# Row statistics one chunk ahead, the row factors spread by transposes of a repeated column, and a reordered start and end of stage 1 in a fused attention and dense block

## The reference

```python
def layernorm(x): m = mean(x); v = var(x); return (x - m) / sqrt(v + 1e-5)

# attention on xn = layernorm(x)
C_q  = xn @ Wq_d + bq_d            # 1024 -> 12
C_kv = xn @ Wkv_d + bkv_d          # 1024 -> 4
q = (C_q @ W_qk + b_qk).reshape(b, s, 32, 4)
scores = einsum('bqhd,bkd->bhqk', q, C_kv) / sqrt(4)
attn = softmax(scores)
V = (C_kv @ Wv_u + bv_u).reshape(b, s, 32, 32)
x = x + einsum('bhqk,bkhd->bqhd', attn, V).reshape(b, s, 1024) @ Wo + bo

# dense layer on layernorm(x)
base = layernorm(x) @ W.T + bias
lora = sum_n (2 * lora_weights[n]) * (layernorm(x) @ A[n].T) @ B[n].T   # 8 x rank 16
x = x + base + lora
```

## Time and profile before

| quantity | value |
|---|---|
| median of 3 runs | 2078.73 us |
| the profiled execution, its own time | 2079.62 us |
| its span | 2077.6 us |
| mean granted clock of TensorE | 0.999 |
| ScalarE busy | 1969.5 us (95%) |
| TensorE busy | 1962.2 us (94%) |
| VectorE busy | 475.6 us (23%) |
| GpSimd busy | 214.9 us (10%) |
| first exponential of attention starts | 105.78 us |

### The profile page before, as it was taken

How to read it: one execution, slowest core, us unless ns; L and a number is a source line. 1 busy time by engine, 2 the same in 40 slices (tenths; PEclk the granted TensorE clock), 3 DMA queues, 4 the chain that set the end, 5 groups by cost and what they waited for, 6 DMA issues and landing times.

```text
span 2077.6 us, 36033 instructions
## 1 busy us (share of the span) xinstructions
PE 1962.2 (94%) x15085; PEld 715.1 (34%) x15085; DVE 475.6 (23%) x1140; ACT 1969.5 (95%) x2185; POOL 214.9 (10%) x220
## 2 busy tenths in 40 slices
PE   7979898999999999999999999999999999999999
PEld 4522222333333333333333333333333333333337
DVE  7713333111121211211121111212111111212115
ACT  5799999999999999999999999999999999999980
POOL 5600000000110002000110001100110001100022
PEclk9999999999999999999999999999999999999999
DMA  8442000000010001000010000100010000100011
GB/s 308 147 137 86 3 26 26 5 25 13 26 35 15 13 26 46 5 13 26 26 35 3 26 25 13 36 15 26 13 46 5 26 13 26 35 15 13 26 41 41
DMA packets 45806, 77.42 MB, mean 37 GB/s; under 512 B 15886, under 2 KB 29766, under 8 KB 45642
## 3 DMA queue, kind: packets, MB, share of 16 engines
q1 hardware_dynamic: 43296, 75.02, 10.7%
q10 hardware_dynamic: 2346, 0.09, 0.1%
HBM read 51.23 MB, written 23.86 MB: 36 GB/s over the span
## 4 chain that ended last, share of the span: by engine, by line
ACT 43%; PE 35%; issue 16%; DVE 0%; DVEq 0%
ACT probs L634 43%; PE ps L914 17%; PE ps L959 10%; PE ps L903 6%; PE ps L948 2%; PE ps L937 0%; PE ps L943 0%; PE ps L775 0%; DVE y L1433 0%; PE ps L1056 0%; PE ps L1052 0%; DVE o_t L1489 0%; ACT o_t L649 0%; ACT o_sb L646 0%; DVE recip L1481 0%
## 5 line engine op out<-in xcount | busy, mean ns | idle before, releaser
L634 ACT ACTIVATE probs<-ps 128x1024 f32<-128x1024 f32 x2048 | 1899.8, 1030 | 17.7 <-PE ps L903 7.1
L914 PE MATMUL ps<-probs,c_wide 128*32 128x512 f32 x8192 | 985.7, 599 | 0.0
L903 PE MATMUL ps<-q_in,key_t 27*128 27x512 bf16 x4096 | 404.2, 385 | 94.1 <-ACT probs L634 90.8
L959 PE MATMUL ps<-w_eff,xn_t 128*128 128x512 f32 x1344 | 394.5, 418 | 0.0
L914 PEld LDWEIGHTS ps<-probs,c_wide 128*32 128x32 f32 x8192 | 212.3, 108 | 424.9 <-issue 220.0
L903 PEld LDWEIGHTS ps<-q_in,key_t 27*128 27x128 bf16 x4096 | 103.0, 91 | 722.7 <-ACT probs L634 715.2
L1433 DVE SCALAR_TENSOR_TENSOR y<-ps,nw,y 128x512 f32<-128x512 f32 x64 | 48.1, 751 | 979.0 <-PE ps L959 967.6
L959 PEld LDWEIGHTS ps<-w_eff,xn_t 128*128 128x128 f32 x1344 | 228.2, 188 | 102.1 <-issue 69.8
L536 POOL TENSOR_TENSOR y<-y,ffn_bias 128x1024 f32<-128x1024 f32 x32 | 76.4, 2388 | 1349.9 <-DVEq L1454 1349.9
L531 POOL TENSOR_TENSOR y<-y,attn_bias 128x1024 f32<-128x1024 f32 x32 | 75.9, 2385 | 463.9 <-DMA y<-in_L_attn_x_dram 463.8
L1417 DVE TENSOR_TENSOR y<-ps,y 128x512 f32<-128x512 f32 x56 | 38.7, 692 | 134.9 <-PE ps L937 134.9
(11 more groups left out here) (168 smaller groups left out, 619.7 us busy)
## 6 DMA issues: line engine op xcount, KB each, us to landing
y<-in_L_attn_x_dram SPq DMA_DIRECT2D x40, 512.0 KB, 4.3
out_dram<-y SPq DMA_DIRECT2D x31, 512.0 KB, 2.7
area<-in_L_attn_x_dram SPq DMA_DIRECT2D x16, 512.0 KB, 9.1
q_in<-q_parts SPq DMA_DIRECT2D x256, 27.0 KB
q_parts<-q_parts_sb SPq DMA_DIRECT2D x48, 128.0 KB, 2.8
xn<-in_L_attn_x_dram SPq DMA_DIRECT2D x8, 512.0 KB, 7.7
y<-in_L_attn_Wo_dram SPq DMA_DIRECT2D x1, 2048.0 KB, 8.6
xn<-in_L_attn_Wo_dram SPq DMA_DIRECT2D x1, 2048.0 KB, 13.3
```

The source lines that it names most:

```text
L634: nc.scalar.activation(probs[:, (c * STEPS + step) % PROBS, bass.ts(pair, 2 * N)], ps[:, 2 * (i % SCORE_SLOTS):2 * (i % SCORE_SLOTS) + 2, ...
L903: last = nc.tensor.matmul(ps[:, at, :], key_t[TILE * h:TILE * h + KEYS, bass.ts(b * KT + kt, P)], q_in[TILE * h:TILE * h + KEYS, g % 2, :] ...
L914: last = nc.tensor.matmul(ps[32 * h:32 * h + 32, SUMS, :], c_wide[:, b * KT + kt, at:at + 32], probs[:, (c * STEPS + step) % PROBS, bass.t ...
L959: last = nc.tensor.matmul(ps[:, SHARED, :], xn_t[:, t % 2, a, kb, :], w_eff[:, b, kb, bass.ts(half, N)], start=(kb + i == 0), stop=(kb == ...
```

## The change

The sections of stage 1 are changed as follows.

1. `statistics` runs one chunk ahead instead of two: DVE's loop for c is now `scale_parts(c-1)`, `split_latents(c-2)`, `statistics(c+1)`.
2. POOL no longer builds the diagonal blocks. PE spreads the factors with four transposes in which one column of `x_r` is read as 128 columns. `deviations_x(c)` waits for `r_ps` where it waited for `diag_ready`.
3. For chunk 0 `spread_r` and `move_r` move from the end of chunk 0 to behind block 1 of chunk 1.
4. The largest latent is no longer taken per chunk from `lat`. It is taken once per batch from the turned latents in `c_wide` (`largest_of_rows`), turned on PE (`turn_largest`), reduced again and spread.
5. The nine weight loads are counted by two semaphores: three by `w_in`, six by `wqk_in`. Only the query bias waits for the six.
6. PE runs `keep_busy` transposes at the start: 16 before anything else and 2, 6 and 4 between the tiles of `turn_first`.
7. At the end, the latents are turned before the queries are made, ACT moves the values first, and the last `split_latents` stands behind the flag, beside the last `split_shift`. The stage 1 buffers lie elsewhere within `probs`, so exponential 3 waits for `lat_split` where exponential 0 did.

```diff
             def deviations_x(c):
...
                 pool.wait_ge(x_measured, c + 1)
                 if c >= 2:
-                    pool.wait_ge(diag_ready, c - 1)
+                    pool.wait_ge(r_ps, c - 1)
...
-                    pool.tensor_tensor(r, a, r, ALU.mult).then_inc(p_r, 1)
-                    pool.wait_ge(p_r, n + 6 + 4 * i)
-                if c:
-                    pool.wait_ge(r_ps, c)
-                pool.tensor_tensor(diag[:, :, :], ident[:, :].unsqueeze(1).to_broadcast([P, TT, P]),
-                                   r.unsqueeze(2).to_broadcast([P, TT, P]), ALU.mult).then_inc(diag_ready, 1)
+                    pool.tensor_tensor(r, a, r, ALU.mult).then_inc(p_r if i < 2 else r_ready, 1)
...
             def spread_r(c):
-                pe.wait_ge(diag_ready, c + 1)
+                pe.wait_ge(r_ready, c + 1)
                 pe.wait_ge(high_ready, c)
-                nc.tensor.matmul(ps[:, 5, :], ones[:, :], diag[:, :, :].rearrange("p t n -> p (t n)"), start=True, stop=True
-                                 ).then_inc(r_ps, 1)
+                for t in range(TT):
+                    last = nc.tensor.transpose(ps[:, 5, bass.ts(t, P)], x_r[:, c % 2, 2, t:t + 1].to_broadcast([P, P]), ident[:, :])
+                last.then_inc(r_ps, 1)
...
+            WARM = (2, 6, 4)
+            keep_busy(16, 5, ident)
...
+                    if t < TT - 1:
+                        keep_busy(WARM[t], 5, ident)
...
-        W_IN = 9 * 16
+        W_IN = 3 * 16
+        WQK_IN = 6 * 16
...
+            def query_bias():
+                pe.wait_ge(wqk_in, WQK_IN)
+                nc.tensor.matmul(ps[:, 6, 0:1], wqk_sb[0:32, :], bqk_sb[0:32, 2:3], start=True, stop=True).then_inc(query_ps, 1)
...
+                    if kb == 1 and c == 1:
+                        spread_r(0)
+                    if kb == 4 and c == 0:
+                        query_bias()
...
-                    if kb == KB - 1:
+                    if kb == KB - 1 and c:
                         spread_r(c)
...
             keep_busy(6, 0)
             sum_parts(CHUNKS - 1)
+            keep_busy(5, 0)
+            turn_latents(CHUNKS - 1, 1)
             queries(CHUNKS - 1)
-            turn_latents(CHUNKS - 1, 1)
+            turn_largest(1, 4)
             keep_busy(2, 0)
-            largest(1, 5)
-            keep_busy(4, 0)
+            largest(1, 4)
+            keep_busy(2, 0)
             pe.wait_ge(caug_ready, START + CHUNKS)
             bounds(1, 6)
...
-                if meanwhile:
-                    ch.then(nc.vector.tensor_reduce(c_max[:, bass.ds(c, 1)], src, AX.X, ALU.max, apply_absolute_value=True))
-                    meanwhile()
-                else:
-                    ch.put(nc.vector.tensor_reduce(c_max[:, bass.ds(c, 1)], src, AX.X, ALU.max, apply_absolute_value=True))
...
+            def largest_of_rows(b):
+                dve.wait_ge(caug_ready, START + (b + 1) * CB)
+                nc.vector.tensor_reduce(c_top[:, b, :], c_wide[:, b * KT:(b + 1) * KT, CW:CW + L].rearrange("p t l -> p l t"),
+                                        AX.X, ALU.max, apply_absolute_value=True).then_inc(c_top_ready, 1)
...
             for c in range(1, CHUNKS):
                 scale_parts(c - 1)
-                if c == 1:
-                    statistics(2)
+                if c == CB + 1:
+                    largest(0, 6)
                 if c == CHUNKS - 2:
                     weigh(0, 6)
-                if 2 <= c < CHUNKS - 1:
+                if c >= 2:
                     split_latents(c - 2, c % 2)
-                if c == CHUNKS - 2:
-                    split_latents(c - 1, 1 - c % 2)
-                if c == CB + 1:
-                    largest(0)
-                if c + 2 < CHUNKS:
-                    statistics(c + 2)
+                if c + 1 < CHUNKS:
+                    statistics(c + 1)
+                if c == CB:
+                    largest_of_rows(0)
...
-            split_latents(CHUNKS - 1, 1, lambda: (largest(1), weigh(1, 5)))
+            largest_of_rows(1)
+            largest(1, 4)
+            weigh(1, 4)
...
-            split_shift(P, 6, shift_split, bound_max[:, 1:2], judge)
+            split_shift(P, 6, shift_split, bound_max[:, 1:2], judge, lambda: split_latents(CHUNKS - 1, 1))
```

More of the change, by code:

```diff
@@ L145, in build_block @@
         nw = sb("nw", [P, 2, 4, TT], F32)
-        c_max = sb("c_max", [P, CHUNKS], F32)
-        c_maxb = sb("c_maxb", [P, B], F32)
+        c_top = sb("c_top", [P, B, L], F32)
+        c_most = sb("c_most", [L, B], F32)
         bound_w = sb("bound_w", [P, B, H], F32)
@@ L660, in _, with keep_busy @@
             pe.wait_ge(const_ok, 4)
+            def keep_busy(times, bank, tile=wqk_sb):
+                for _ in range(times):
+                    nc.tensor.transpose(ps[:, bank, 0:P], tile[:, :], ident[:, :])
+            WARM = (2, 6, 4)
+            keep_busy(16, 5, ident)
             def first_weights():
@@ L666, in first_weights @@
                 nc.tensor.matmul(ps[:, 7, 0:1], bias_row, ones[0:1, 0:1], start=True, stop=True)
-                nc.tensor.matmul(ps[:, 7, 1:2], wqk_sb[0:32, :], bqk_sb[0:32, 2:3], start=True, stop=True)
                 last = nc.tensor.matmul(ps[:, 7, 32:32 + KB * 32], ones[:, :], w_down[:, :, :].rearrange("p k n -> p (k n)"),
@@ L727, in queries, with turn_largest @@
                 nc.tensor.matmul(ps[:, 7, :], wqk_sb[:, :], down_part[:, :], start=True, stop=True).then_inc(q_ps, 1)
+            def turn_largest(b, bank):
+                pe.wait_ge(c_top_ready, b + 1)
+                nc.tensor.transpose(ps[0:L, bank, 0:P], c_top[:, b, :], ident[:, :]).then_inc(c_turned, 1)
             def largest(b, bank):
-                pe.wait_ge(c_max_ready, b + 1)
-                if b == B - 1:
-                    pe.wait_ge(high_ready, CHUNKS)
-                nc.tensor.matmul(ps[:, bank, 0:1], sel_latent[:, :], c_maxb[:, b:b + 1], start=True, stop=True
+                pe.wait_ge(c_most_ready, b + 1)
+                nc.tensor.matmul(ps[:, bank, P:P + 1], sel_latent[0:L, :], c_most[:, b:b + 1], start=True, stop=True
                                  ).then_inc(bound_w_ps, 1)
@@ L756, in stage1 @@
                         down(c - 1, 1)
+                    if kb == 1 and c == 1:
+                        spread_r(0)
+                    if kb == 2 and c == CHUNKS - 3:
+                        pe.wait_ge(caug_ready, START + c - 1)
+                        turn_largest(0, 6)
                     if kb == 2 and c == CHUNKS - 2:
@@ L769, in stage1 @@
                         queries(c - 1)
-                    if kb == KB - 1:
+                    if kb == KB - 1 and c:
                         spread_r(c)
-            def keep_busy(times, bank):
-                for _ in range(times):
-                    nc.tensor.transpose(ps[:, bank, 0:P], wqk_sb[:, :], ident[:, :])
             for c in range(CHUNKS):
@@ L791, in _ @@
             pe.wait_ge(min_ready, 1)
-            nc.tensor.matmul(ps[0:1, 4, 0:P], bound_max[:, B:B + 1], ident[:, :], start=True, stop=True).then_inc(tight_ps, 1)
+            nc.tensor.matmul(ps[0:1, 4, 2 * P:3 * P], bound_max[:, B:B + 1], ident[:, :], start=True, stop=True).then_inc(tight_ps, 1)
             keep_busy(4, 0)
+            pe.wait_ge(high_ready, CHUNKS)
             pe.wait_ge(tight_ok, 1)
@@ L1170, in split_shift @@
                 if then:
+                    beside()
                     dve.wait_ge(first_shift, SHIFT_BLOCKS * 16)
@@ L1174, in split_shift @@
                 ch.then(nc.vector.tensor_tensor(rest, shift, parts[:, 0, :], ALU.subtract))
-                if beside:
+                if beside and not then:
                     beside()
```

57 lines of the change are left out of this document (34 added, 23 removed).

## The result

The changed kernel takes 2073.71 us (median of 7 runs, 2071.58 to 2074.32), the kernel before 2079.61 (7 runs): ratio 0.997, 95% interval 0.996 to 0.9979. It is faster by 5.9 us where 14.4 were forecast, and 2073.71 is 0.7 above the range. The profiled execution of after took 2071.58 (span 2069.7), the fastest of its seven, that of before 2079.62 (span 2077.6). About 0.55 of them can be named. In all twelve other traces with the new order of statistics the step from chunk 1 to 2 took 9.17 to 9.21 us, and only in this one 8.62. In those twelve VectorE's last product of `split_latents` takes 1.54 us, beside GpSimd's L513; here it takes 0.75.

What follows compares the result with a forecast made beforehand. Stage 1 before the first exponential was taken as serial to attention, its period set by DVE (9.85 us), PE next (8.98). Gains 5.5 + 3.1 + 4.3 + 0.4 + 0.4 + 0.7 = 14.4 us gave 2064.3, range 2060.5 to 2073.

Steps and rivals of the forecast that it cites:

- chunk 0 to 1: Step of 11.88 us in stage 1: one chunk's statistics instead of two between the `scale_parts`, so 8.8, gain 3.1.
- four steady steps: `sum_parts` of chunks 1 to 5, 39.46 us: falls to 35.2, gain 4.3; ends 1.9 to 5.2.
- step 5 to 6: Stage 1 step of 10.05 us, bound by PE: loses 0.42 of spreading, `turn_largest` adds 0.15 elsewhere; gain 0.4.
- What waits for the later statistics: Query split and store behind later `deviations_x`: both fit, counted zero, 1 us for each kept in the range.
- the second of the two waits named there: ACT's next use of the query buffer at 17.7; six stores issued by 14, landing by 17, little to spare.
- The end: `sum_parts(7)` to first exponential, 10.81 us: maximum of bounds at 5.9 instead of 7.05; gain 0.7, from 0 to 1.7.
- The start: Until `sum_parts` of chunk 0, at 25.53: faster PE and earlier weights bring it to 20.0, 5.5 us earlier.
- The period: Steady chunk step: loops of 8.56 (PE), 8.6 (DVE) and about 8.5 (ACT) give 8.8 us.
- the lock: DVE and GpSimd lock each other out at L1227; in the new order it takes 0.9 us instead of 1.44.
- That idle transposes don't raise PE's speed: Rival, chance 0.20: PE stays at half speed at the start, `sum_parts(0)` at 27.2, median 2071.5 us.
- That ACT waits for the stores: Rival, 0.11, shared with DVE waiting for POOL: period stays at 9.5, five steps 0.7 more, 2067.8 us.
- That the factor is late: Rival, 0.04: look-ahead of one chunk too short for POOL's chain, paid in 7 chunks; 2083 us at 9.3.

Runs made afterwards that it cites:

- misc: Changed kernel with the five loads of biases, factors and lora_a issued behind the query stores of chunks 2 and 3; 2071.47 us, ratio 0.9962.
- m_after: Changed kernel with one idle transpose on TensorE as a marker, between the branch behind the flag and the wait for q_in; 2073.26 us, one run.
- the padded kernels: Semaphore increments at TensorE's start: 96 on the changed kernel (2080.13 us), 96 with five loads moved (2076.73), 55 without start's idle transposes (2074.74).
- misc_far: Changed kernel, five loads behind query stores, 19 more idle transposes, the 31 from last `sum_parts` to branch made 64-column f32 matmuls; 2067.29 us, ratio 0.9941.
- misc_far6: As `misc_far`, with 6 and 2 of the 64-column f32 matmuls ahead of the flag in place of 12 and 4; 2068.01 us, ratio 0.9942.
- nowarm_pad55: Changed kernel without the idle transposes at the start, with 55 semaphore increments at TensorE's start, branch again at place 1190; 2074.74 us, one run.
- compact: Changed kernel with idle transposes replaced by wide products of the same length, 60 instructions fewer; 2072.62 us, ratio 0.9967.
- misc_compact: Changed kernel with wide products for idle transposes and the five loads behind the query stores of chunks 2 and 3; 2069.59 us, ratio 0.9952.
- nowarm: Changed kernel without the idle transposes at the start (16, and 2, 6 and 4 between the tiles); 2075.32 us, one run.
- place: Changed kernel with 19 more idle transposes where TensorE waits anyway, branch at place 1228; 2072.5 us, ratio 0.9965.
- m_before: Kernel before with one idle transpose on TensorE as a marker behind the branch that follows the flag; 2077.75 us, one run.
- misc_pad96: Changed kernel with the five loads behind the query stores and 96 semaphore increments at TensorE's start; 2076.73 us, ratio 0.9994.

## Why the prediction was wrong, step by step

| step | forecast us | measured us |
|---|---|---|
| start to `sum_parts(0)` | -5.5 | -4.64 |
| chunk 0 to 1 | -3.1 | -3.27 |
| four steady steps | -4.3 | -4.67 |
| step 5 to 6 | -0.4 | +1.48 |
| step 6 to 7 | -0.4 | -0.10 |
| `sum_parts(7)` to flag | -0.7 | -0.79 |
| flag to first exponential | 0 | +3.48 |
| from there to the end | 0 | +0.47 |
| sum | -14.4 | -8.04 |

**The steps that failed.** "What waits for the later statistics ... I count zero": ACT did wait for a query store, the second of the two waits named there. The length was the error. I let the stores land 3 us after their issue; behind five loads they took 6.1 to 7.6. It cost 1.9 us in this profile and more where the wait is 3.90. `misc` showed it: with the loads moved, the stores land in 3.2 and the step is 9.5. The 1 us that the range kept for it was too little.

"The end": the term up to the flag was right to 0.1. Beyond it I took the jump and the first scores as fixed: the flag to the first exponential stands at nothing in the sum. The change makes PE's program 98 places longer up to the branch, and that moved the branch into a place from which the code behind it comes 3.3 us late (3.60 us of branch in place of 0.37). Then PE, idle for 4.7 us, ran at half speed, and 0.15 and 0.47 more were lost; the second is net of the same kind of fall in the profiled before, and would be 0.62 by the spans alone. `m_after`, the padded kernels, `misc_far` and `misc_far6` showed it. No row of the trace of before has such a stop; what I could have seen is that a branch over 325 instructions stands behind the flag, and that a longer program shifts it. Store and jump together are 5.8 of the 6.4 us missed.

**Mis-sized.** The start by 0.9. Everything up to it came as worked out: the last tile turned at 11.5 (forecast 11.3), chunk 1's turning at 16.04 (16.0), `spread_r(0)` at 18.00 (18.0), the statistics' end at 19.3 (19.1). But DVE's next step came late. VectorE in order of time, kernel after:

```profile
18.88 0.43 DVE L1229 BATCH_NORM_AGGREGATE x_mv<-stats 128x2 f32<-128x12 f32 x4
20.14 0.69 DVE L1239 TENSOR_TENSOR down_part<-ps,o_sb 128x512 f32<-128x512 f32 x1 [0.83 <-DVEq L1147]
```

The pause of 0.83 us between the two was 0.42 in the earlier trace rows, and of that I had put in 0.2. Why it is 0.4 longer here than there, no run shows.

**Right.** The period, within 0.1: 8.70 for 8.8, and the four transposes of the repeated column in 0.60. TensorE, kernel after:

```profile
26.04 0.60 PE L720 MATMUL ps<-ident,x_r 128*128 128x128 f32 x4
```

A column read 128 times loads like 128 columns. The factor was never late. L1250 took 0.73 to 0.75 in after (0.74 to 1.61 before), so the lock went as I had it there, and better than the 0.9 that I took. It showed once in a place that I had not counted, the 1.54 of `key_t` in chunk 1 to 2.

**The rivals.** That idle transposes don't raise PE's speed is refuted: the first tile's transposes take 0.93 at 6.13, the second's 0.66, and in `nowarm_pad55` nothing but transposes stands ahead of the rise. The rule of the Trainium skill, "TensorE: Matmul & The Clock Gate", "Part 4: PE-mode transpose", that transposes don't count for the clock, does not hold for the f32 transposes of this run. That ACT waits for the stores was a rival at 0.11, with 0.7 us in each of five steps; it came once, with 1.9. That the factor is late did not happen.

The lock shows from the other side. GpSimd in order of time, kernel after, a step that ran beside L1250 (55.41, 0.73 long):

```profile
55.11 0.20 POOL L500 TENSOR_TENSOR x_r<-x_r 128x4 f32<-128x4 f32 x1
55.40 0.80 POOL L502 TENSOR_SCALAR x_r<-x_r 128x4 f32<-128x4 f32 x1
```

L502 takes 0.80 in place of 0.20 and ends 0.06 after VectorE. That is what "SBUF — State Buffer", "Who interferes with whom", of the Trainium skill says of the loser, and the small steps bear it: GpSimd was busy 6.65 of 8.61.

## What to carry to other kernels

When an edit lets a buffer's reader come earlier, work out the landing of the transfers from what stands ahead of them on their queue at that moment, not from their usual time. When it adds or takes instructions ahead of a far jump, expect the first instruction behind it to move by some 3 us either way, and read the branch's own row (0.37 or 3.60 us here) to see it; filler in places where the engine waits anyway can buy it back. A pause between two instructions of one engine is a term of the sum like any other.

## What the runs showed of the hardware that was not expected

- A taken branch over 325 instructions on TensorE took 0.36 to 0.46 us in ten traces and 3.48 to 3.88 in six. From the flag to the first instruction behind it that is 1.3 to 1.6 us and 4.5 to 4.9. The same lateness shows as a stop of 2.0 to 2.7 us in straight code (`compact`, `misc_compact`, `nowarm`).
- A semaphore increment on TensorE cost 0.15 us (96 of them let it start at 15.44 us, 55 at 9.35).
- After an idle time of 2.8 to 4.7 us TensorE was at half speed for several us (`place` from 68.85, granted clock 0.54; after from 97.17, 0.62). After ones of 1.4 to 1.6 it went either way: half speed at once in `misc_far6` (1.58), some 2 us later in before (1.38), not at all in `m_before` (1.37) and `misc_pad96` (1.57). The length of the idle time does not decide it there, and what does is open.
- f32 products of 64 columns are no cheaper filler than transposes of 128: twelve took 2.89 us (`misc_far`), twelve transposes 1.53 (after).
